# Expert rows scattered by slot into a DRAM buffer, loaded in quarters and turned by VectorE, in a mixture-of-experts kernel on one core

## The reference

```python
def _moe_forward(x, gate_w, w_gate_up, w_down, shared_w_gate_up, shared_w_down):
    x2 = x.reshape(-1, orig_shape[-1])
    gu_s = x2 @ shared_w_gate_up.T
    g_s, u_s = jnp.split(gu_s, 2, axis=-1)
    shared_out = jax.nn.silu(g_s) * u_s @ shared_w_down.T
    logits = x2 @ gate_w.T
    probs = jax.nn.softmax(logits, axis=-1)
    topk_vals, topk_idx = jax.lax.top_k(probs, TOP_K)
    topk_vals = topk_vals / jnp.sum(topk_vals, axis=-1, keepdims=True)
    combine = jnp.sum(jax.nn.one_hot(topk_idx, NUM_EXPERTS) * topk_vals[..., None], axis=1)
    gu = jnp.einsum('th,eih->eti', x2, w_gate_up)
    g, u = jnp.split(gu, 2, axis=-1)
    act = jax.nn.silu(g) * u
    out_e = jnp.einsum('eti,ehi->eth', act, w_down)
    moe_out = jnp.einsum('eth,te->th', out_e, combine)
    return (moe_out + shared_out).reshape(orig_shape)

x = x + tanh(g_xattn) * attention(layernorm(x), ctx, ...)
x = x + tanh(g_ffn) * _moe_forward(layernorm(x), ...)
```

## Time and profile before

| | |
|---|---|
| median of 3 runs | 1397.36 us (1397.26 to 1397.74) |
| the profiled execution's own time | 1397.51 us |
| its span, first to last instruction | 1395.8 us |
| granted TensorE clock, mean | 0.999 |
| PE / DVE / ACT / POOL busy | 99% / 72% / 37% / 26% |
| the experts, by the trace of PE | from 1198.18 to about 1345 us |

### The profile page before, as it was taken

How to read it: one execution, slowest core, us unless ns; L and a number is a source line. 1 busy time by engine, 2 the same in 40 slices (tenths; PEclk the granted TensorE clock), 3 DMA queues, 4 the chain that set the end, 5 groups by cost and what they waited for, 6 DMA issues and landing times.

```text
span 1395.8 us, 26753 instructions
## 1 busy us (share of the span) xinstructions
PE 1382.0 (99%) x8757; PEld 1121.7 (80%) x8758; DVE 1000.4 (72%) x2135; ACT 514.6 (37%) x1117; POOL 358.0 (26%) x374
## 2 busy tenths in 40 slices
PE   9999999999999999999999999999999999999998
PEld 7888887888888887888887888888787888777777
DVE  6444456888888888888888888888688746244458
ACT  5333444333333434343333333343434331222242
POOL 1121223221212121212211121212122100367646
PEclk9999999999999999999999999999999999999999
DMA  6544431111111111111101111111123244555548
GB/s 220 189 128 143 128 109 44 39 42 31 49 31 43 39 42 32 43 40 41 43 30 47 36 42 32 49 31 42 54 72 98 99 151 174 188 196 165 165 154 298
DMA packets 91238, 125.52 MB, mean 90 GB/s; under 512 B 7184, under 2 KB 57360, under 8 KB 90896
## 3 DMA queue, kind: packets, MB, share of 16 engines
q1 hardware_dynamic: 83632, 99.70, 22.7%
q0 software_dynamic: 7520, 24.65, 5.3%
HBM read 86.84 MB, written 37.49 MB: 89 GB/s over the span
## 4 chain that ended last, share of the span: by engine, by line
PE 79%; DVE 3%; issue 1%; DMA 1%; ACT 0%; DVEq 0%; POOL 0%; SPq 0%; ACTq 0%
PE ps L609 19%; PE ps L611 18%; PE ps L610 18%; PE ps L1004 6%; PE ps L696 5%; PE ps L743 4%; PE ps L1020 3%; PE ps L728 2%; PE ps L999 1%; DVE acc L1960 1%; DVE acc L1967 1%; DMA y<-ybuf 1%; PE ps L917 1%; PE ps L751 0%; PE ps L1051 0%
## 5 line engine op out<-in xcount | busy, mean ns | idle before, releaser
L506 POOL CAST vth<-vt 128x256 fp32r<-128x256 f32 x64 | 25.4, 397 | 541.4 <-PE ps L743 539.4
L1194 ACT CAST ah<-ps 128x256 fp32r<-128x256 f32 x256 | 83.4, 383 | 187.5 <-PE ps L611 181.0
L609 PE MATMUL ps<-hT,w0h 128*128 128x512 f32 (+1 forms) x384 | 152.2, 396 | 0.0
L611 PE MATMUL ps<-hT,w0h 128*128 128x512 f32 (+1 forms) x384 | 149.9, 390 | 0.0
L610 PE MATMUL ps<-hT,w0l 128*128 128x512 f32 (+1 forms) x384 | 149.6, 390 | 0.0
L500 POOL TENSOR_TENSOR qr<-qv,mhalf 128x8 f32<-128x8 f32 x64 | 105.1, 1642 | 151.5 <-DVE qv L1560 124.3
L1511 DVE TENSOR_TENSOR acc<-ps,acc 128x512 f32 (+1 forms) x128 | 88.0, 687 | 56.6 <-PE ps L611 56.4
L1160 ACT COPY qs<-ps 128x512 f32<-128x512 f32 x128 | 75.3, 588 | 122.6 <-PE ps L611 122.6
L1172 ACT ACTIVATE pb<-pb 128x256 f32<-128x256 f32 x128 | 48.3, 418 | 167.0 <-DVE pb L1578 166.9
L609 PE MATMUL ps<-w0l,ah 128*128 128x512 f32 x256 | 105.6, 413 | 0.0
L609 PE MATMUL ps<-w1l,ah 128*128 128x512 f32 x256 | 104.9, 410 | 0.0
(11 more groups left out here) (250 smaller groups left out, 3216.1 us busy)
## 6 DMA issues: line engine op xcount, KB each, us to landing
wraw<-in_w_att SPq DMA_DIRECT2D x64, 256.0 KB, 2.7
vbuf<-vo SPq DMA_DIRECT2D x16, 512.0 KB, 3.3
kbuf<-ko SPq DMA_DIRECT2D x16, 512.0 KB, 3.8
kt<-kbuf SPq DMA_DIRECT2D x32, 256.0 KB, 2.9
vt<-vbuf SPq DMA_DIRECT2D x64, 128.0 KB, 2.2
wgu<-in_w_gu SPq DMA_DIRECT2D x4, 2048.0 KB, 9.0
y<-ybuf SPq DMA_DIRECT2D x16, 512.0 KB, 7.1
xt<-in_x SPq DMA_DIRECT2D x16, 256.0 KB, 4.2
```

What stands on the lines that cost most here:

```text
L609: pe.matmul(dst, l_hi, r_lo, start=first, stop=False)
L611: return pe.matmul(dst, l_hi, r_hi, start=False, stop=last)
L1194: act.copy(ah[:, bp, :, b2, :], pv_view(bp, b2)).then_inc(a_hi, 1)
```

## The change

The rows of a block no longer come by a gather from `h2buf`. A second DRAM buffer, `xbuf`, holds the rows in slot order. As soon as DVE has the slots as integers (`sli`), POOL scatters each of the 16 token tiles twice into `xbuf`, by first and second choice: 32 indirect DMAs. Their source is four tiles `rows0` to `rows3` that SP loads back from `h2buf`; these tiles lie in the memory of `act_raw` of the last group, so DVE waits for all scatters before `shared_in(3, 0)`. SP loads a block by four DMAs, one per quarter of the columns, each into 32 partitions of `xg`; with the columns of `h2_tile` written in another order (`by_quarter`), one VectorE transpose in 32x32 squares per block (`turn_rows`) writes `xgT`. PE's `expert_T` and ACT's `xT_out` are gone. So that slots without a token hold finite numbers, SP copies input rows into all of `xbuf` during the attention loop, 512 KB per pair of steps. `sidx` is gone, `didx` stays. PE's turn of the logits moves ahead by half a `gate_up`, and DVE's `shared_in(1, 1)` behind the row maximum. DVE's block does now, in this order: `gated(b)`, `ye` of b-1, the turn of b+2, `acteT` of b. Several semaphores are merged to make room for new ones, which changes no order.

```diff
+    xbuf = nc.dram_tensor("xbuf", [(STEPS - NC) * P, D], F32, kind="Internal").ap()
...
+    x_rows = xbuf.rearrange("(b g i) (q n) -> b q i g n", g=4, i=32, q=4)
...
+            rows = [sb(f"rows{q}", [P, D], F32, a) for q in range(4)]
...
             with sp.Fori(0, (STEPS - NC) // 2) as d:
                 for odd in range(2):
                     next_loads(d, odd)
+                sp.dma_start(x_pair[d], x[0:2]).then_inc(x_in, 16)
...
+            def load_rows(n):
+                if n >= 4:
+                    sp.wait_ge(rows_out[n % 4], 32 * (n // 4))
+                sp.dma_start(rows[n % 4][:], h2_t[n]).then_inc(rows_in[n % 4], 16)
+
+            def load_block(b, j):
+
+                if not isinstance(b, int) or b >= 3:
+                    sp.wait_ge(xgT_done, b - 2)
+                for q in range(4):
+                    src = x_rows[b, q] if isinstance(b, int) else x_rows[bass.ds(b, 1), q].rearrange(
+                        "a i g n -> (a i) g n")
+                    sp.dma_start(xg[j % 3][32 * q:32 * q + 32, :].rearrange("p (g n) -> p g n", g=4), src).then_inc(
+                        xg_in[j % 3], 16)
...
+            sp.wait_ge(lgt_done, 1)
+            for n in range(4):
+                load_rows(n)
             load_gate_up(1)
+            for n in range(4, 12):
+                load_rows(n)
             load_gate_up(2)
-            sp.wait_ge(slot_ok, 1)
+            for n in range(12, 14):
+                load_rows(n)
+            sp.wait_ge(slot_ok, 2)
             sp.wait_ge(sidx_done, 1)
             load_down(4)
+            load_rows(14)
             load_down(12)
+            load_rows(15)
+            for q in range(4):
+                sp.wait_ge(rows_out[q], 32 * 4)
+            for b in range(3):
+                load_block(b, b)
             load_gate_up(3, done=wgu_last)
+            for b in range(3, 11):
+                load_block(b, b)
...
+            pool.wait_ge(slot_ok, 1)
+            for n in range(NT):
+                pool.wait_ge(rows_in[n % 4], 32 + 16 * (n // 4))
+                for z in range(2):
+                    pool.indirect_dma_start(xbuf, bass.IndirectOffsetOnAxis(sli[:, z, n:n + 1], 0),
+                                            rows[n % 4][:], None).then_inc(rows_out[n % 4], 16)
...
-            gate_up(3, 3, (0,))
-            pe.wait_ge(act_f, 17)
-            expert_T(0, 0, 0)
-            expert_T(1, 0, 1)
+            pe.wait_ge(act_f, 16)
+            gate_up_half(3, 3, 0, (0,))
+            gate_up_half(3, 3, 1, (0,)).then_inc(w_free, 1)
             e0, loads0 = expert_of(0, early=True)
-            gate_up(3, 3, (1,))
+            for u in range(2):
+                gate_up_half(3, 3, u, (1, 2, 3))
...
-                if not isinstance(b, int) or b + 2 < NB:
-                    expert_T(b + 2, 2 * six, j + 2)
...
-            link(dve.tensor_copy(sli[:], slf[:]))
+            dve.tensor_copy(sli[:], slf[:]).then_inc(slot_ok, 1)
...
-            for it in range(4):
+            for q in range(4):
+                dve.wait_ge(rows_out[q], 32 * 4)
+            for it in range(3):
                 shared_in(3, it)
+
+            def turn_rows(b, q, rounds, j):
+
+                dve.wait_ge(xg_in[j % 3], 64 * rounds + 64 * (j // 3) + 64)
+                if not isinstance(b, int) or b >= 2:
+                    dve.wait_ge(eg_done, b - 1)
+                dve.transpose(xgT[q][:].rearrange("p k (g i) -> p g k i", g=4),
+                              xg[j % 3][:].rearrange("p (g j k) -> p g k j", g=4, k=KD)).then_inc(xgT_done, 1)
+
+            dve.wait_ge(w_free, 1)
+            for b in range(2):
+                turn_rows(b, b, 0, b)
+            shared_in(3, 3)
```

More of the change, by code:

```diff
@@ L297, in h2_tile, with by_quarter, in_order @@
             return h2_first[:, n, :] if n < 4 else h2[n % 4][:]
+        def by_quarter(t):
+            return t.rearrange("p (m k) -> p k m", k=KD)
+        def in_order(t):
+            return t.rearrange("p (k m) -> p k m", k=KD)
         def group_of(n):
@@ L563, in split_down @@
                 pool.tensor_tensor(dn_lo[:, cs], dn_raw[:, cs], dn_hi[:, cs], ALU.subtract).then_inc(shd_lo, 1)
-            for b in range(6):
-                gather(b)
             pool.wait_ge(didx_ok, 1)
-            for b in range(6, NB):
-                gather(b)
-                scatter(b - 6)
-                if b >= 16 and b % 4 == 0 and b < 48:
-                    split_down(b // 4 - 4)
-            for b in range(NB - 6, NB):
+            for b in range(NB):
                 scatter(b)
+                if b >= 10 and b % 4 == 2 and b < 42:
+                    split_down(b // 4 - 2)
             for n in range(NT):
@@ L750, in transpose_h2 @@
                 for k in range(KD):
-                    mm = pe.transpose(PS[bank][:, k * P:(k + 1) * P], h2_tile(n)[:, k * P:(k + 1) * P], ident[:])
+                    mm = pe.transpose(PS[bank][:, k * P:(k + 1) * P], by_quarter(h2_tile(n))[:, k], ident[:])
                 mm.then_inc(h2T_done, 1)
@@ L761, in gate_up_half @@
                     mm.then_inc(gu_done, 1)
+                return mm
             def outputs(r, w_before, w_o, o_ready=None, turn=True):
@@ L962, in _ @@
             logits(3)
-            gate_up(1, 1)
+            gate_up(1, 1, (0,))
             pe.wait_ge(lg_evac, 4)
@@ L968, in _ @@
             mm.then_inc(lgt_done, 1)
+            gate_up(1, 1, (1,))
             gate_up(1, 2)
             gate_up(1, 3)
-            pe.wait_ge(tri_ok, 1)
+            pe.wait_ge(const_dve, 7)
             pe.wait_ge(rank_in, 1)
@@ L993, in _ @@
                 gate_up(3, it)
-            def expert_T(b, rounds, j):
-                pe.wait_ge(xg_in[j % 3], 16 * rounds + 16 * (j // 3) + 16)
-                for k in range(KD):
-                    mm = pe.transpose(PS[j % 2][:, k * P:(k + 1) * P], xg[j % 3][:, k * P:(k + 1) * P], ident[:])
-                mm.then_inc(xgT_done, 1)
             def expert_gate_up(b, q, e, ks):
@@ L1265, in normalise @@
                     act.wait_ge(h2_stored[n % 4], 16 * (n // 4) + 16)
-                act.activation(h2_tile(n), acc[:, n, :], ACT.Identity, bias=nb3[:, n:n + 1],
+                act.activation(by_quarter(h2_tile(n)), in_order(acc[:, n, :]), ACT.Identity, bias=nb3[:, n:n + 1],
                                scale=rs3[:, n:n + 1]).then_inc(h2_act, 1)
@@ L1379, in _ @@
             act_round(0, 0)
-            act_block(NB - 3, 0)
-            act_block(NB - 2, 1)
+            for b in range(NB - 3, NB):
+                act_block(b, b % 2)
             act.wait_ge(eg_done, NB)
@@ L1821, in _ @@
             shared_in(1, 0)
-            shared_in(1, 1)
             links = [0]
@@ L1842, in _ @@
             dve.tensor_tensor(ra[:], ra[:], over_e(rsm[:]), ALU.subtract).then_inc(rt_sub, 1)
+            shared_in(1, 1)
             dve.wait_ge(rt_exp, 1)
@@ L1953, in _ @@
             for b in range(NB - 3, NB):
-                dve_block(b, b % 2)
+                dve_block(b, b // 6, b % 6)
+            rows_out_of(NB - 1, (NB - 1) % 2)
             def combine(n):
```

132 lines of the change are left out of this document (67 added, 65 removed).

## The result

The changed kernel takes 1446.8 us (median of four runs, 1444.65 to 1448.59) against 1397.55 for the kernel before (four runs, too): a ratio of 1.035, interval 1.0332 to 1.0368. The forecast had the sign and not the size: 1406, with a range to 1429. The profiled execution after has a span of 1444.5 us and took 1446.51.

A forecast was written before the change was run, and what follows sets the result against it. PE was taken to bound the kernel, busy 99% of the span. Later start +17.5, block 3 +4, clock +2 and faster steps -15.0 sum to +8.5 us on 1397.5: 1406, own range 1399 to 1415, overall 1393 to 1429.

The forecast's parts named there:

- the start's, +17.5 and 2: Ahead of the experts: they start 17.5 us later, waiting for the last scatter; 2 us more for PE's clock after idling.
- the steps', -15.0: 46 expert steps fall from 3.155 to 2.83 us, set by DVE's order with a turn of 0.71: 15.0 us gained.
- the rival with the slow turn: In the expert steps: the strided VectorE turn takes 1.15 us, the step 3.27, total 1426; chance 0.22.
- row loads, whose delay I took at 4: Before the experts: row loads behind weight loads on the queue delay the last scatter by 4 us (0 to 8).
- the prediction's own 300 GB/s: Expert block loads: DMA rate when full estimated at about 300 GB/s, against 185 GB/s needed, so loads cost nothing.
- The clock's term: Last two `gate_up` pieces before the experts: after PE idles 18 us, a lower clock costs 2 us (0 to 11).
- Nothing that I find brings them earlier: Ahead of the scatters: the integer slots stay ready at 1157.41 us, as before the change.
- The bound of 7 us for TensorE's turns: PE's 64 turns of `h2_tile`, now reading every fourth number, could cost 7 us; taken at 0.
- the first pair of the earlier trace: Sums over 128 numbers: 382 ns at 128-byte spacing, 272 for neighbours; 0.86 ns per element, giving a 1.15 us turn.
- Block 3, +4: Early expert steps: block 3's load, behind the last 2 MB weight load, comes late and costs 4 us.
- Quick scatters: Before the experts: scatters issue 0.97 us apart without the pause, experts start 4.2 late, total 1392; chance 0.12.
- Late quarter loads: In the expert steps: late block loads hold the step at 3.155 us, total 1421; chance 0.07.

The follow-up runs named there:

- loads_act: Changed kernel with four weight loads issued by ACT on its own queue instead of SP's: 1440.8 us, ratio 1.0315.
- weights_behind: Changed kernel with the 2 MB and two 1 MB weight loads moved behind the last row load: 1443.7 us, ratio 1.033.
- turn_plain: Changed kernel with VectorE's turn of the expert rows reading neighbouring numbers instead of every fourth (other values result): 1432.5 us, ratio 1.0249.
- turn_last: Changed kernel with VectorE copying `acteT` of block b+1 before it turns block b+3, not after: 1427.6 us, ratio 1.0218.
- rows_apart: Changed kernel with row tiles in memory no shared piece writes, and without VectorE's wait for the scatters before `shared_in(3, 0)`: 1436.3 us, ratio 1.0285.
- tuned: Changed kernel with `acteT` copied first, row tiles apart, plain row order reordered by stores, last gate-up weights behind row loads, last shared weight in four loads: 1414.9 us.

## Why the prediction was too low

The direction and both mechanisms were right: the wait of VectorE for the last scatter, and VectorE's order as the limit of a step. What failed are the sizes of the two main terms: the start's, +17.5 and 2, measured 37.7, and the steps', -15.0, measured +7.2 beside block 3's 4.7. Two things, besides, were costed at nothing that are not free. Even the rival with the slow turn, 1426, is 20 us short, since it kept the start's term.

- *The start, +17.5 and 2 for the clock.* Measured 37.7. The last scatter landed 18.4 us later than forecast: 6.8 by the slots, 0.9 from the slots to the first scatter, 5.6 by the first four beside the one-hot products, and 5.3 by row loads, whose delay I took at 4 and which came to 9.3 beyond the pause. Small differences take 0.2 off. The forecast's range for this delay ended at 8, and its reason, weights ahead on SP's queue, is not enough: `loads_act` takes them off that queue and keeps 9.4 us of waits, `weights_behind` puts them behind the row loads and leaves 1.7. Nor were the bytes held against the time: from the slots to the last landing, 58 us, 16.0 MB moved, 8.4 of them by the scatters. At the prediction's own 300 GB/s, used there for the block loads only, that is an estimated 53 us, where its start had 46 (1157.41 to 1203.8); 300 is no limit, though, since the stretch from 1200 to 1212 moved 403. The clock's term held: 12.66 - 10.96 = 1.7, after the 29.8 us without a product, over which the granted clock fell to 0.50, the lower of its levels (1.2 GHz).
- *"Nothing that I find brings them earlier", and nothing to make them later.* The copies in the attention and the strided normalising and turning on TensorE were costed at nothing; alone they put the slots back by 4.1 and 2.2 us in one trace each, and in the changed kernel the two places lost 3.3 and 3.5. The bound of 7 us for TensorE's turns was there, the strided writes of ScalarE and VectorE when they normalise were not considered at all.
- *The steps, -15.0.* The taken price of the turn, 0.71, failed; the bound from the first pair of the earlier trace rows, 1.15, was near (1.10). The rival built on it had the step at 3.27; it measured 3.17. `turn_plain` shows that the formula was right: with 0.70 the steps are 2.78 to 2.93 for a forecast 2.83. The round is 0.34 us longer than forecast, and 46 x 0.34 is 15.6 of the 41 us that were missing.
- *Block 3, +4.* The first two steps take 11.0 instead of 6.3: 4.7.
- *The loop's turns* were not in the sum: 0.5 us at each of five (3.7 instead of 3.2), 2.5 in all. Before, the four turns on TensorE stood at this place; the remainder of 0.4 in `turn_last`, where VectorE is ahead, says that TensorE itself is late there, and why is not shown. With these, 18.8 of the 22.9 us are named by which the steps are longer than forecast (157.1 against 46 x 2.83 + 4 = 134.2). The rest lies in steps of 3.2 to 3.4 and some longer early ones; in the eighth, 3.88, VectorE waits 1.4 us for an earlier scatter of `ye`.
- *The rivals.* Quick scatters: none was under 1.26 apart. Late quarter loads: after the start VectorE waits for one load only, 3.3 us, block 3's.

What stays open is what moves the end of the attention. In the profiled executions that share that part with the changed kernel, the first normalised tile starts between 1063.3 and 1070.3, against 1062.2 before, though all have the same copies; so the 4.1 of one trace is no better than a few us, and 2.4 is what the medians give. From that tile to the slots the traces agree: 95.0 us before and with the copies alone, 97.1 with the stride, 95.8 to 96.1 in the three versions without it. Only the changed kernel and `rows_apart` have 98.6 there, and the 1.5 us more are not explained. A version that gathers blocks as before and only turns them on VectorE was not tried: the gather would need a further pass through DRAM or SBUF.

## What to carry to other kernels

A step that saves 0.3 us forty-six times is worth 15 us only if what feeds it is no dearer: count the bytes that the new path moves between the moment when its addresses are known and the moment when the first result is wanted, and hold them against the DMA engines' time there, not against the mean. Where a transpose can be moved to another engine, choose the order of the data so that neither its read nor the writer's store steps by 16 bytes from number to number; and put the short copy that TensorE waits for ahead of the long operation that nobody waits for yet, which here was worth more (19 us) than the price of the stride (14 us). The two gains don't add: with the copy first the step is 2.71 with the stride and 2.70 without it (`tuned`).

## What the runs showed of the hardware

- A VectorE transpose of 128x512 float32 takes 0.70 us when it reads neighbours and 1.10 when it reads every fourth number. ScalarE writing every fourth number takes 1.28 instead of 0.80, and a TensorE weight load that reads them 0.21 instead of 0.14.
- An indirect DMA that takes POOL 0.96 us took 1.8 to 2.6 beside VectorE operations of 1.7 to 2.3 us on two SBUF operands.
- Copies from DRAM to DRAM at a DMA share of 0.2 (0.14 without them) put a TensorE-bound loop back by 2.4 us by the medians and 4.1 in one trace, part of it as waits for nothing but "issue".
- A 256 KB load that landed 2.5 us after its issue at the quickest took up to 10.7 beside weight loads of 1 and 2 MB on the same queue, up to 9.4 with these on another queue, and up to 4.6 with only scatters beside it.
